# Attention and mixture of experts on one core: one ScalarE step moved ahead of another, and row statistics and norm factors cut in three parts

## What is computed

```python
x = x + tanh(g_xattn) * (softmax(q k^T / 8) v @ w_out + b_out)   # q from layernorm(x), k and v from the context (120 rows a batch); 16 heads of 64
x = x + tanh(g_ffn) * moe(layernorm(x))                          # 8 experts of 1024, the best 2 of each row, silu
```

## Time and profile before

| what | us |
|---|---|
| median of 3 runs | 527.07 |
| lowest and highest | 525.77, 527.6 |
| the profiled execution's own time | 530.4 |
| its span | 528.7 |

### The profile page before, as it was taken

One profiled execution on the slowest core, in us unless ns is written; L12 is line 12 of the kernel. 1 busy time (PEld: TensorE's weight loads), 2 busy tenths in 40 slices (PEclk: granted clock), 3 DMA queues, 4 the chain that ended last, 5 costly groups with the idle time before them and its releaser, 6 DMA issues.

```text
span 528.7 us, 17694 instructions
## 1 busy us (share of the span) xinstructions
PE 486.9 (92%) x6692; PEld 436.4 (83%) x6692; DVE 363.8 (69%) x866; ACT 371.2 (70%) x577; POOL 369.9 (70%) x414
## 2 busy tenths in 40 slices
PE   2889689999999999999688999989999999999993
PEld 2877568888888878888468899979999999999993
DVE  5799899898988989998887757553344443444431
ACT  1788989999899989988764577544555655556551
POOL 5369779798999999899968766564554645455432
PEclk9999989999999999999989999998999999999998
DMA  7953416154360725325073638886888888788712
GB/s 289 398 195 95 167 38 204 51 185 140 99 208 34 243 67 182 124 95 195 24 268 110 255 118 303 251 254 150 260 226 245 241 226 265 212 256 239 211 22 31
DMA packets 35061, 94.87 MB, mean 179 GB/s; under 512 B 4507, under 2 KB 24475, under 8 KB 27645
## 3 DMA queue, kind: packets, MB, share of 16 engines
q1 hardware_dynamic: 25812, 82.79, 45.2%
q0 software_dynamic: 8592, 10.81, 11.9%
q10 hardware_dynamic: 576, 0.14, 0.1%
HBM read 74.45 MB, written 19.28 MB: 177 GB/s over the span
## 4 chain that ended last, share of the span: by engine, by line
PE 66%; POOL 12%; DVE 9%; ACT 5%; issue 5%; DMA 3%; POOLq 0%; SPq 0%; ACTq 0%; DVEq 0%
PE st_bank L1707 20%; PE j_bank L1707 15%; PE o_bank L1707 14%; PE j_bank L1852 4%; POOL pT L618 3%; POOL stage L663 3%; PE max_pair L1908 2%; PE j_bank L1713 2%; PE st_bank L1929 2%; POOL table L637 2%; PE j_bank L1811 2%; DMA stage<-in_w 2%; PE max_pair L1970 1%; DMA w2s<-in_wq 1%; PE j_bank L1876 1%
## 5 line engine op out<-in xcount | busy, mean ns | idle before, releaser
L1541 DVE SCALAR_TENSOR_TENSOR hT<-hf,h_scale,hT 128x512 f16<-128x512 f32 x78 | 58.9, 758 | 87.2 <-ACT hT L1016 87.1
L1707 PE MATMUL st_bank<-xsT,w_tile 128*128 128x128 f16 x1872 | 113.3, 221 | 2.1 <-DVE xsT L1535 1.4
L1707 PEld LDWEIGHTS st_bank<-xsT,w_tile 128*128 128x128 f16 x1872 | 109.6, 99 | 3.0 <-DVE xsT L1535 1.6
L730 POOL DMA_INDIRECT out<-yt,row_of x39 | 62.7, 1607 | 57.0 <-DVE yt L1550 42.3
L1010 ACT ACTIVATE hf<-st_bank,z_scale 128x512 f32<-128x512 f32 x78 | 52.9, 678 | 45.2 <-PE st_bank L1707 39.2
L618 POOL TENSOR_TENSOR pT<-pT 120x512 f16<-120x512 f32 x64 | 77.3, 1223 | 7.3 <-ACT pT L884 7.1
L1707 PE MATMUL o_bank<-w2s,hT 128*128 x600 | 69.7, 273 | 0.3 <-DVE yt L1550 0.3
L1016 ACT ACTIVATE hT<-hf,h_scale 128x512 f16<-128x512 f32 x78 | 56.3, 722 | 10.5 <-PE o_bank L1707 4.2
L1707 PEld LDWEIGHTS o_bank<-w2s,hT 128*128 128x128 f16 x600 | 57.6, 98 | 7.1 <-issue 0.8
L883 ACT ACTIVATE pT<-st_bank,exp_bias,logit_scale 120x512 f32<-120x512 f32 x64 | 50.0, 781 | 14.0 <-PE st_bank L1932 12.7
L663 POOL TENSOR_SCALAR stage<-stage,upw 128x512 f32<-128x512 f32 x32 | 56.5, 1766 | 4.1 <-ACT w_hi L983 4.1
(11 more groups left out here) (226 smaller groups left out, 1022.7 us busy)
## 6 DMA issues: line engine op xcount, KB each, us to landing
w_tile<-w_split SPq DMA_DIRECT2D x39, 1024.0 KB, 6.3
stage<-in_w SPq DMA_DIRECT2D x16, 1024.0 KB, 5.1
w_split<-w_hi SPq DMA_DIRECT2D x8, 512.0 KB, 2.8
w_split<-stage SPq DMA_DIRECT2D x8, 512.0 KB, 3.8
out<-x SPq DMA_DIRECT2D x17, 128.0 KB, 3.2
xin<-in_x SPq DMA_DIRECT2D x8, 256.0 KB
w2s<-in_wkv SPq DMA_DIRECT2D x2, 1024.0 KB, 11.9
xres<-in_x SPq DMA_DIRECT2D x16, 128.0 KB, 2.1
```

Of the source, the lines that this page charges most:

```text
L730: pool.indirect_dma_start(out=out[0:rows], out_offset=bass.IndirectOffsetOnAxis(row_of[:, t:t + 1], 0), in_=yt[t % XG][:], in_offset=None, ...
L1541: nc.vector.scalar_tensor_tensor(out=hT[par][:, 1, 4 * a:4 * a + 4, :], in0=hf[par][:, 512 * a:512 * a + 512].rearrange("p (c n) -> p c n" ...
L1707: ins = pe.matmul(out, lhs[i](a), rhs[i](c), start=(i == 0 and a + c == 0), stop=(i == n - 1 and a == 1))
```

## The change

Only three things differ in the lists of instructions; the loops are written out from the seventh step on, which leaves the order as it was.

1. On ScalarE `x_high(b)` stands one place earlier in each period, ahead of `weight_sum(b - 1, 0)`, for b = 1 to 7.
2. Tiles 6 to 15 are cut into 6 to 9 and 10 to 15. The statistics of tiles 6 to 9 keep their place on VectorE; those of tiles 10 to 15 come behind `norm2_rows(0)`, two periods later. SyncE loads the two parts with two DMAs in place of one.
3. On GpSimd the factors of tiles 6 to 9 are made behind `p_low(0, 2, 1)`, three places later than those of tiles 6 to 15 were, and the factors of tiles 10 to 15 behind `p_low(2, 2, 1)`, ahead of `scatter(0, 1)`.

```diff
-RESTS = ((NT, 4), (NT + 4, TT - NT - 4))
+RESTS = ((NT, 4), (NT + 4, 4), (NT + 8, TT - NT - 8))
...
-            sp.dma_start(x_rest[1], x_v[:, RESTS[1][0]:sum(RESTS[1]), :]).then_inc(x_all_in[1], 16)
+            for i in range(1, len(RESTS)):
+                sp.dma_start(x_rest[i], x_v[:, RESTS[i][0]:sum(RESTS[i]), :]).then_inc(x_all_in[i], 16)
...
-            for p in range(-8, B + 3):
+            for p in range(-8, 0):
                 p_low(p + 6, 2, 1)
+                norm_factors(p + 6, 2)
+                norm_factors(p + 4, 3)
                 scatter(p + 4, 1)
                 norm2_factors(p + 5)
                 p_low(p + 6, 3, 0)
...
-                norm_factors(p + 7, 2)
                 p_low(p + 7, 2, 0)
...
-                act.wait_ge(norm_scales, 1 + (b > 0) + (b > 2))
+                act.wait_ge(norm_scales, 1 + (b > 0) + (b > 2) + (b > 4))
...
-                        for j in range(2):
+                        for j in range(len(RESTS)):
                             act.wait_ge(stats_done[j], 1)
...
                 exps(p, 2, 0)
                 exps(p, 2, 1)
+                x_high(p + 2)
                 weight_sum(p + 1, 0)
-                x_high(p + 2)
                 weight_sum(p + 1, 1)
                 weight_diagonals(p + 1)
...
                 x_stats(p + 1, 2)
                 norm2_rows(p - 1)
+                x_stats(p - 1, 3)
```

More of the change, by code:

```diff
@@ new lines, in _ @@
+            scatter(5, 0)
+            p_low(7, 2, 1)
+            scatter(5, 1)
+            norm2_factors(6)
+            p_low(7, 3, 0)
+            p_low(7, 3, 1)
+            tile_gather(7, 2)
+            tile_gather(7, 3)
+            tile_gather(7, 4)
+            residual(7, 1)
+            tile_gather(7, 5)
+            residual(7, 0)
+            scatter(6, 0)
+            scatter(6, 1)
+            norm2_factors(7)
+            tile_add(7, 0)
+            tile_gather(7, 6)
+            tile_gather(7, 7)
@@ L792, in _ @@
+            tile_add(7, 1)
+            tile_gather(7, 8)
+            scatter(7, 0)
+            scatter(7, 1)
+            tile_add(7, 2)
+            find_rows(7, 1)
+            tile_add(7, 3)
+            tile_gather(7, 9)
+            tile_gather(7, 10)
+            tile_gather(7, 11)
+            tile_add(7, 4)
+            tile_add(7, 5)
+            tile_gather(7, 12)
+            tile_add(7, 6)
+            tile_gather(7, 13)
+            tile_add(7, 7)
+            tile_add(7, 8)
             for t in range(LISTED - 1, TILES):
@@ new lines, in _ @@
+            exps(7, 0, 1)
+            split_high(7, 1, 0)
+            v_high(7, 1)
+            o_high(6, 0, 0)
+            exps(7, 1, 0)
+            o_high(6, 1, 1)
+            exps(7, 1, 1)
+            o_high(6, 0, 1)
+            gate_ratio(5)
+            exps(7, 2, 0)
+            exps(7, 2, 1)
+            exps(7, 3, 0)
+            tile_high(7, 0)
+            exps(7, 3, 1)
+            tile_high(7, 1)
+            load_silu(7)
+            o_high(7, 1, 0)
+            tile_hidden(7, 0, 0)
@@ new lines, in _ @@
+            add_residual(5, 0)
+            count_tiles(4, 0, 0)
+            norm_o(6, 1, 1)
+            count_tiles(4, 0, 1)
+            count_tiles(4, 0, 2)
+            max_rows(7, 0)
+            weight_scales(7)
+            norm_o(6, 2, 0)
+            row_max(7, 2)
+            norm_o(6, 2, 1)
+            split_low(7, 0, 0)
+            o_low(6, 1, 0)
+            v_low(7, 0)
+            norm_o(6, 3, 0)
+            split_low(7, 0, 2)
+            norm2_rows(5)
+            norm_o(6, 3, 1)
@@ new lines, in _ @@
+            tile_scales(7, 0, 2)
+            add_residual(6, 1)
+            tile_gates(7, 0)
+            add_residual(6, 0)
+            norm_o(7, 1, 1)
+            tile_low(7, 0)
+            norm_o(7, 2, 0)
+            tile_low(7, 1)
+            norm_o(7, 2, 1)
+            o_low(7, 1, 0)
+            tile_h_low(7, 0, 0)
+            norm_o(7, 3, 0)
+            norm2_rows(6)
+            norm_o(7, 3, 1)
+            choose(6)
+            o_low(7, 0, 0)
+            o_low(7, 1, 1)
+            o_low(7, 0, 1)
@@ new lines, in _ @@
+            slots(6)
+            route(6)
+            tile_h_low(7, 0, 1)
+            add_residual(7, 1)
+            add_residual(7, 0)
+            tile_low(7, 2)
+            tile_h_low(7, 1, 0)
+            tile_h_low(7, 1, 1)
+            tile_gated(7, 0)
+            tile_low(7, 3)
+            tile_h_low(7, 2, 0)
+            norm2_rows(7)
+            tile_gated(7, 1)
+            choose(7)
+            tile_h_low(7, 2, 1)
+            tile_low(7, 4)
+            add_turns(7, 0)
+            slots(7)
@@ new lines, in _ @@
+            values(7, 3, 0)
+            norm2_T(6)
+            values(7, 3, 1)
+            logits(6)
+            o_T(7, 0, 0)
+            o_T(7, 1, 1)
+            tile_up(7, 1, 1)
+            o_T(7, 0, 1)
+            ranks(6)
+            out_product(7, 1, 0)
+            out_product(7, 1, 1)
+            out_product(7, 0, 0)
+            tile_T(7, 2)
+            out_product(7, 0, 1)
+            tile_T(7, 3)
+            tile_down(7, 0)
+            tile_up(7, 2, 0)
+            tile_T(7, 4)
@@ new lines, in _ @@
+            tile_down(7, 1)
+            tile_T(7, 5)
+            norm2_T(7)
+            tile_up(7, 2, 1)
+            logits(7)
+            tile_up(7, 3, 0)
+            tile_up(7, 3, 1)
+            ranks(7)
+            tile_down(7, 2)
+            tile_up(7, 4, 0)
+            tile_T(7, 6)
+            tile_T(7, 7)
+            tile_up(7, 4, 1)
+            tile_down(7, 3)
+            tile_up(7, 5, 0)
+            tile_up(7, 5, 1)
+            tile_down(7, 4)
+            tile_T(7, 8)
+            tile_up(7, 6, 0)
```

368 lines of the change are left out of this document (200 added, 168 removed).

## The result

The changed kernel takes 540.82 us (median of four, 539.06 to 541.81) against 527.34 us beside it: ratio 1.0248 with a 95% interval of 1.0209 to 1.0288, so it is slower, by 13.5 us between the medians and by 13.1 by the ratio. (One of the four executions of before, at 535.82, was in a slower state; the ratio is of the others.) The forecast of 535.8 had the side right and the size too small; 540.82 lies just inside its range of 527.5 to 541.0.

The account below looks back on a forecast made before the run. The prediction took TensorE to set the pace, with no engine having room. Its terms 1.4 + 1.1 + 0.8 + 2.1 + 3.3 = 8.7 us, on the median of 527.07, gave 535.8, range 527.5 to 541.0.

Parts of the forecast that it names:

- the rows asked for: Signs named: ScalarE idle about 2.5 and 1.5 us, diagonals' product at 39.3, late statistics near 110, product-with-v wait about 4.
- The first term: First two periods, high part ahead of weight sum: 1.9 us late, 0.46 given back, 1.4 us lost.
- gives back: Second period, behind the diagonals' product: TensorE's one wait of 0.46 us takes up part of the 1.9 us.
- I take no new drop: First two periods: no added TensorE clock drop; 0.8 us for one went only into the upper end.
- The third term: Third period, high part ahead of weight sum: ScalarE stands still 1.45 us, 1.1 us lost.
- the later ones: Fourth to seventh periods, same swap: fourth hidden behind part 3, fifth and seventh 0.4 each, sixth covered; 0.8 us together.
- The period of batch 6: Sixth period: ScalarE waits 1.50 us for the load of a weight sum anyway, which covers the swap.
- The statistics: VectorE, six tiles' statistics behind `norm2_rows(0)` at about 107 us: 2.5 less 0.4 of waiting, 2.1 us lost.
- The factors: GpSimd's full stretch, six-tile block ahead of a scatter: the product-with-v wait grows from 0.7 to 4.0, 3.3 us lost.
- Overlapping losses: Rival: third-period, later and statistics losses absorbed in the longer wait for GpSimd; 4.7 us lost, 531.8; chance 0.30.
- Faster, through the second period: Rival: second-period high part on time, TensorE's waits and clock drop vanish; 3.5 us gained, 523.6; chance 0.13.
- Slower through the clock: Rival: two more clock drops, before the diagonals' product and after the product-with-v wait, 0.8 each; 537.4; chance 0.08.

Follow-up runs that it names:

- first swap alone: Kernel before with only batch 1's high part moved ahead of the weight sum of expert 0: 530.97 us against 527.50.
- all swaps alone: Kernel before with the high part ahead of the weight sum in all seven periods and nothing else: 534.47 us against 527.45.
- later swaps alone: Kernel before with the high part ahead of the weight sum only from the third period on (batches 3 to 7): 530.77 us against 526.97.
- factors alone: Kernel before with the factors of six tiles late, ahead of the second scatter; statistics in two groups at their old place, no swap: 533.62 us against 527.45.
- the wait was filled: The late-factors kernel with 60 small matrix products on TensorE ahead of its wait for the probabilities' low part: 532.85 us against 533.62 unfilled.
- factors in a pause: The late-factors kernel with the six tiles' factors one period earlier, where GpSimd waits: 528.45 us against 527.45 for the kernel before.
- second swap: Kernel before with only batch 2's high part moved ahead of the weight sum of expert 1: 527.36 us against 527.50.
- same waits filled: The first-swap and late-factors kernels, each with small products on TensorE ahead of its long wait: 533.17 and 532.85 us, against 530.97 and 533.62 unfilled.
- control: Kernel before with 44 more small products on TensorE in an early wait of 8.32 us that nothing hangs on: 530.39 us against 529.68.
- before with its waits filled: Kernel before with small products on TensorE in two second-period waits and ahead of the tile loop's first row product: 530.72 us against 526.97.

## Why the prediction was right, and by how much it fell short

**The side and the three mechanisms were right**, and the rows asked for came. ScalarE idles 2.50 us before the first high part and 1.45 before the third. The first diagonals' product stands at 38.80, which is 39.5 with the earlier start taken out, where 39.3 was forecast. The statistics stand at 111.05 with a TensorE wait for VectorE of 1.09 behind them; the product with v waits 3.33 us.

**The first term failed in size.** For the first two periods the forecast took "1.4, because the diagonals' place behind two sums excludes most of the gain". The changed kernel lost 3.3 there, the first swap alone 3.46, and all swaps alone 2.3. Two statements and one choice were behind the 1.4. The lateness of 1.9 is right: with the clock held it is 1.94. That TensorE "gives back" its wait of 0.46 in the second period did not help the changed kernel: the wait is gone, but the products ahead of it take longer at the lower clock (1.09 and 2.70 us, against 0.63 and 2.27 in before), and the later time goes through. Where the clock was 1.00 there, with all swaps alone, 1.3 us came back. Nor was it the only wait there: another of 1.06 us at 74.52 follows in before, and it didn't shrink (1.30 in the changed kernel). And the choice, "I take no new drop, as the rows show one only behind two waits in a row", is wrong: a single wait of 2.67 us (2.69 with the first swap alone) had a drop behind it, worth 1.5 us at that place.

**The third term was nearly right, the later ones too small.** 1.1 was forecast for the third period, 1.30 measured with the later swaps alone. For the four others together 0.8 was forecast. Swapped without the rest of the change they cost 2.3: in each, ScalarE's wait of some 1.57 us costs 0.3 to 0.7. In the changed kernel the first of them is hidden behind the factors, as forecast, and the other three cost 1.8. The period of batch 6, which a wait for a load was to cover, lost least, 0.31.

**The statistics**: 2.1 forecast. The changed trace loses 1.74 between the third period's transposes of normed rows and the routing behind it; by the medians it is 1.1.

**The factors**: the growth of the wait was right for the factors alone (3.3 forecast, 4.07 - 0.73 = 3.34 measured; in the changed kernel 3.33 - 0.73 = 2.60), the price was not. Alone they cost 6.2 us, of which 2.6 are the clock behind the wait by the trace, though the time fell by only 0.8 us when the wait was filled. In the changed kernel's own profile this drop is missing: after a wait of 3.33 us the clock stays at 1.00, and the loss there is 3.1. That profile is of the fastest of its executions, at 539.06; whether the slower ones have the drop isn't shown. The rows name no engine for this wait: "issue" stands for time whose cause the profile doesn't show, in the earlier trace rows as in the earlier trace rows, so that GpSimd waited only for its own DMAs was more than the row says (0.6 us more went to VectorE's routing). That TensorE waits for GpSimd's low part is borne out by the runs: it ends at 142.43 in the changed kernel, the product starts at 142.53, and with the factors in a pause the wait is 0.73 again.

**The rivals.** Overlapping losses, to which I gave 0.30, is refuted: the parts add, within what the intervals leave open. "Faster, through the second period" failed where the forecast said, at the diagonals, and not only because of the first period: with ScalarE on time the second swap still gains nothing, as it was run, with the clock low behind the diagonals. "Slower through the clock" had the right mechanism and too small a price: 0.8 a drop, measured 1.5 and 2.6. The Trainium skill (TensorE: Matmul & The Clock Gate, Part 1: The HAM clock gate) states that an array without activity falls back to half rate. The traces agree behind the waits of 2.67 and 4.07 us, and with the same waits filled the clock held; behind the 3.33 us of the changed profile they don't.

In sum, by kernels with one part each: first swap 3.5, second 0, later 3.8, factors 6.2, statistics 1.1, together 14.6 against 13.5 for the whole. In the forecast these were 1.4 for the first two, 1.9, 3.3 and 2.1. The forecast of 8.7 counted the waits. Against those runs it left out the clock behind two of them, 1.5 + 2.6, and 1.5 us in the later periods, had 1.0 too much for the statistics, and the remaining 1.3 is spread over the terms (0.5 of it the wait that was not given back). The clock's share is what the traces show at the two places; the total times didn't confirm it. In the changed kernel's one profile the same list reads 3.3, 1.3, 1.7, 3.1 and 1.8: the 11.2 us. No kernel that was tried beats the one before.

## What to carry to other kernels

When a step is moved ahead of another on a full engine, ask whether its input is there: if not, the step behind it loses its cover, and what comes after can be late by the whole step, as in the first period (in the later ones by 0.3 to 0.7 us of a wait of 1.57). A wait of TensorE that grew from 0.6 to 2.7 us, or from 0.7 to 4.1, was priced twice in these runs, once as the wait and once as the slow products behind it; take the second price from a row at the lower clock, as an upper end that may not come. And a small block of work is free in an engine's pause and can cost more than its length in a full stretch (6.2 us for 3.3 here), so look for the pause first.

## What I had not expected

- A drop of the clock is not worth the same everywhere. Behind the late factors it cost 2.6 us, in the second period of the kernel before nothing, because the next wait there took it up (0.46 became 1.40).
- Nor does it follow from the length of the wait alone: it came behind 2.67 and 4.07 us, and not behind 3.33 us in the changed profile. The same three waits of TensorE, 1.6, 1.4 and 1.5 us from about 252 us on, have a drop behind them in the profiles of before and of the control, and none in that of before with its waits filled.
- The loop over the tiles can take back what the front has gained. In the control, GpSimd waits 3.12 us for the entries it wrote before it can read them, against 2.49 in before, and TensorE then waits 1.81 us for a tile. GpSimd's timeline of the control:

```profile
331.92 0.94 POOL L696 DMA_INDIRECT found<-table,blk  x1 [3.12 <-DMA table<-entry,slot]
```

That wait of GpSimd's does not decide it by itself: in before with its waits filled it is 2.34 us, and TensorE waits 1.65. What the six profiles with a wait of 1.65 us or more for the tile share is that this read starts 0.6 to 1.5 us later than in before, measured against TensorE's last transposes of normed rows; in the seven others it is 0.1 us later at most. What makes it late was not settled. It limits what the total time of a single-part kernel can tell: two kernels whose fronts differ by 2 us can come out alike.
